# Row sums of a two-layer graph network folded and turned by VectorE instead of TensorE

## The reference

```
h = relu(layernorm(x))
x = x + adj @ (h * (u >= 0.1) / 0.9)
h = relu(layernorm(x))
x = x + adj @ (h @ W) + b
```

## Time and profile before

| what | us |
|---|---|
| median of 3 runs | 932.2 (932.02 to 932.36) |
| the profiled execution's own time | 932.63 |
| its span, first to last instruction | 930.8 |
| TensorE busy | 900.5 (97%) |
| VectorE busy | 175.6 (19%) |
| ScalarE busy | 23.8 (3%) |
| loads of `adj`, 340 of 1 MB | 391 GB/s on average over the span |

### The profile page before, as it was taken

How to read it: one execution, slowest core, us unless ns; L and a number is a source line. 1 busy time by engine, 2 the same in 40 slices (tenths; PEclk the granted TensorE clock), 3 DMA queues, 4 the chain that set the end, 5 groups by cost and what they waited for, 6 DMA issues and landing times.

```text
span 930.8 us, 10203 instructions
## 1 busy us (share of the span) xinstructions
PE 900.5 (97%) x4480; PEld 356.8 (38%) x4480; DVE 175.6 (19%) x343; ACT 23.8 (3%) x52; POOL 35.6 (4%) x32
## 2 busy tenths in 40 slices
PE   2789999999999999999999999999999999999998
PEld 0224333333334444444444444444444444444444
DVE  5513123132022112021200100200100100200223
ACT  2100000000000000000000000000000000000000
POOL 5900000000000000000000000000000000000000
PEclk9999999999999999999999999999999999999999
DMA  9999999999999999999999999899999999999993
GB/s 370 421 421 421 421 421 421 421 421 420 421 422 421 421 421 420 421 418 404 395 391 359 347 381 395 324 374 352 362 346 376 366 415 400 370 358 421 386 423 155
DMA packets 50828, 363.55 MB, mean 391 GB/s; under 512 B 5680, under 2 KB 5712, under 8 KB 6752
## 3 DMA queue, kind: packets, MB, share of 16 engines
q1 hardware_dynamic: 50688, 362.83, 96.8%
q0 software_dynamic: 96, 0.07, 0.0%
HBM read 360.78 MB, written 2.10 MB: 390 GB/s over the span
## 4 chain that ended last, share of the span: by engine, by line
PE 89%; DMA 10%; SPq 1%; issue 0%; DVE 0%; DVEq 0%
PE banks L583 47%; PE row_sums L572 36%; DMA blocks<-in_adj 10%; PE banks L578 4%; PE turned L643 1%; SPq L363 1%; PE turned L630 1%; SPq L357 0%; SPq L356 0%; DVE rows L532 0%; DVEq L274 0%
## 5 line engine op out<-in xcount | busy, mean ns | idle before, releaser
L583 PE MATMUL banks<-blocks,features 128*64 128x512 f32 x2048 | 670.0, 592 | 1.2 <-DMA blocks<-in_adj 1.2
L572 PE MATMUL row_sums<-blocks,features 128*64 128x512 f32 x1880 | 604.9, 596 | 25.9 <-DMA blocks<-in_adj 25.7
L583 PEld LDWEIGHTS banks<-blocks,features 128*64 128x64 f32 x2048 | 226.6, 137 | 261.9 <-issue 261.9
L572 PEld LDWEIGHTS row_sums<-blocks,features 128*64 128x64 f32 x1880 | 197.7, 138 | 272.2 <-issue 260.8
L509 DVE TENSOR_TENSOR acc<-acc,banks 128x512 f32<-128x512 f32 (+1 forms) x108 | 74.2, 687 | 625.9 <-PE banks L583 568.5
L578 PE MATMUL banks<-blocks,features 128*64 128x512 f32 x168 | 72.5, 592 | 0.0
L578 PEld LDWEIGHTS banks<-blocks,features 128*64 128x64 f32 x168 | 23.0, 137 | 24.2 <-issue 24.2
L430 ACT ACTIVATE sums_sb<-row_sums 128x512 f32<-128x512 f32 (+1 forms) x16 | 9.5, 595 | 749.8 <-PE row_sums L572 375.1
L481 DVE TENSOR_TENSOR rows<-rows,turned 128x256 f32<-128x256 f32 x16 | 6.7, 421 | 68.1 <-PE turned L630 68.1
L389 POOL TENSOR_SCALAR acc<-acc 128x512 f32<-128x512 f32 (+1 forms) x9 | 19.0, 2110 | 6.3 <-DMA acc<-in_u 5.7
L514 DVE TENSOR_TENSOR ahead<-ahead,banks 64x512 f32<-64x512 f32 x21 | 14.4, 685 | 0.7
(11 more groups left out here) (30 smaller groups left out, 72.9 us busy)
## 6 DMA issues: line engine op xcount, KB each, us to landing
blocks<-in_adj SPq DMA_DIRECT2D x340, 1024.0 KB, 10.3
rows<-in_x SPq DMA_DIRECT2D x2, 1024.0 KB, 7.7
acc<-in_u SPq DMA_DIRECT2D x2, 1024.0 KB, 9.9
out<-rows SPq DMA_DIRECT2D x8, 256.0 KB, 2.0
pair_w<-in_w POOLq DMA_DIRECT2D x2, 16.0 KB, 5.9
bias<-in_b POOLq DMA_DIRECT2D x1, 32.0 KB, 5.1
```

What stands on the lines that cost most here:

```text
L572: return nc.tensor.matmul(row_sums[at, s % 2, :], features[:, k * TILES + j, 0:D], tile_of(parts, j), start=first and t.n == row_first[s][ ...
L583: return nc.tensor.matmul(banks[at, t.sum.bank, :], features[:, t.k * TILES + j, D:2 * D], tile_of(parts, j), start=t.n == t.sum.first and ...
```

## The change

TensorE no longer folds or turns the rows of layer 1. ScalarE copies only the upper half (64 partitions) to `sums_sb`. VectorE adds the lower half to it (`folded`), transposes in squares of 32 x 32 into a PSUM bank (`squares`, which is the first bank of the former `turned`, now `finished`), and adds the squares to `rows` in eight additions of 32 partitions x 128 elements. `join_ahead` now writes into `ahead`; where the joined half is the upper one (even rows of 2 to 9), ScalarE's copy waits for it. The constant `fold` goes. `turn_pair` keeps its matmuls.

```diff
             for s in range(BLOCKS):
-                act.wait_ge(part_used, PARTS * (max(row_last[s]) + 1))
+                if s in ahead_done and s % 2 == 0:
+                    act.wait_ge(row_joined, joined_by[s])
+                    upper = ahead[D:P, s // 2 - first_ahead, :]
+                else:
+                    act.wait_ge(part_used, PARTS * (max(row_last[s]) + 1))
+                    upper = row_sums[D:P, s % 2, :]
                 if s >= 2:
-                    act.wait_ge(turned_ready, s - 1)
-
-                at = slice(s % 2 * D, s % 2 * D + D) if s in ahead_done else slice(0, P)
-                nc.scalar.activation(sums_sb[at, s % 2, :], row_sums[at, s % 2, :], ACT.Copy).then_inc(row_copied, 1)
+                    act.wait_ge(row_folded, s - 1)
+                nc.scalar.activation(sums_sb[:, s % 2, :], upper, ACT.Copy).then_inc(row_copied, 1)
...
-                bank = turned[:, s % 2, 0:TILES * D].rearrange("p (t d) -> p t d", d=D)
-                dve.wait_ge(turned_ready, s + 1)
-                nc.vector.tensor_tensor(mine, mine, bank, ALU.add).then_inc(turned_taken, 1)
-                dve.wait_ge(turned_taken, s + 1)
+                dve.wait_ge(row_copied, s + 1)
+                dve.wait_ge(part_used, PARTS * (max(row_last[s]) + 1))
+                lower = row_sums[0:D, s % 2, :]
+                if s in ahead_done:
+                    dve.wait_ge(row_joined, joined_by[s])
+                    if s % 2 == 1:
+                        lower = ahead[0:D, s // 2 - first_ahead, :]
+                if s:
+                    dve.wait_ge(row_turned, s)
+                nc.vector.tensor_tensor(folded[:, :], lower, sums_sb[:, s % 2, :], ALU.add).then_inc(row_folded, 1)
+                dve.wait_ge(row_folded, s + 1)
+                if s:
+                    dve.wait_ge(row_placed, s * (D // SQ) * (P // SQ))
+                nc.vector.transpose(squares, folded[:, :]).then_inc(row_turned, 1)
+                dve.wait_ge(row_turned, s + 1)
+                for f in range(D // SQ):
+                    part = squares[f * SQ:(f + 1) * SQ, :].rearrange("p (t a f) -> p t a f", t=TILES, f=SQ)
+                    for a in range(P // SQ):
+                        to = mine[a * SQ:(a + 1) * SQ, :, f * SQ:(f + 1) * SQ]
+                        nc.vector.tensor_tensor(to, to, part[:, :, a, :], ALU.add).then_inc(row_placed, 1)
+                dve.wait_ge(row_placed, (s + 1) * (D // SQ) * (P // SQ))
...
-                if s >= 2:
-                    dve.wait_ge(turned_ready, s - 1)
-                nc.vector.tensor_tensor(sums_sb[at, s % 2, :], row_sums[at, s % 2, :],
-                                        ahead[at, s // 2 - first_ahead, :], ALU.add).then_inc(row_joined, 1)
+                mine = ahead[at, s // 2 - first_ahead, :]
+                nc.vector.tensor_tensor(mine, mine, row_sums[at, s % 2, :], ALU.add).then_inc(row_joined, 1)
...
             for n in range(END + 2):
                 if n < END:
                     multiply(items[n])
-                if n - 1 in row_end:
-                    turn_row(row_end[n - 1])
```

More of the change, by code:

```diff
@@ L28 @@
 BIAS_ROW = 8
+SQ = 32
 DROP = 0.1
@@ L288, in bass_gnn @@
         ahead = sb("ahead", [P, max(ahead_done) // 2 - first_ahead + 1, BLK])
-        sums_sb = sb("sums_sb", [P, 2, BLK])
-        fold = sb("fold", [P, D])
+        sums_sb = sb("sums_sb", [D, 2, BLK])
+        folded = sb("folded", [D, BLK])
         pair_w = sb("pair_w", [P, 2 * D])
@@ L309, in bass_gnn @@
         row_sums = ctx.enter_context(nc.psum_tensor("row_sums", [P, 2, BLK], f32))
-        turned = ctx.enter_context(nc.psum_tensor("turned", [P, 2, BLK], f32))
+        finished = ctx.enter_context(nc.psum_tensor("finished", [P, 2, BLK], f32))
+        squares = finished[0:D, 0, :]
         banks = ctx.enter_context(nc.psum_tensor("banks", [P, SUM_BANKS, BLK], f32))
@@ L318, in bass_gnn @@
         cleared = sem("cleared")
-        constants = sem("constants")
         warm = sem("warm")
@@ L333, in bass_gnn @@
         row_joined = sem("row_joined")
-        turned_ready = sem("turned_ready")
-        turned_taken = sem("turned_taken")
+        row_turned = sem("row_turned")
+        row_folded = sem("row_folded")
+        row_placed = sem("row_placed")
+        finished_ready = sem("finished_ready")
+        finished_taken = sem("finished_taken")
         sum_added = sem("sum_added")
@@ L367, in _ @@
                 sp.wait_ge(rows_ready, n + 1)
-                sp.wait_ge(turned_taken, BLOCKS + n + 1)
+                sp.wait_ge(finished_taken, n + 1)
                 sp.dma_start(out[:, t, :], rows[:, t, :]).then_inc(stored, 16)
@@ L374, in _ @@
             nc.gpsimd.memset(eps[:, :], EPS).then_inc(cleared, 1)
-            nc.gpsimd.memset(fold[:, :], 0.0).then_inc(cleared, 1)
             nc.gpsimd.memset(pair_w[:, :], 0.0).then_inc(cleared, 1)
[L377 to L382, removed]
+            pool.wait_ge(cleared, 2)
             pool.dma_start(pair_w[0:D, 0:D], w).then_inc(weights_arrived, 16)
@@ L527, in pair_of_rows @@
                 mine = rows[:, 2 * p * TILES:(2 * p + 2) * TILES, :].rearrange("p (r t) d -> p r t d", r=2)
-                bank = turned[:, n % 2, :].rearrange("p (t r d) -> p r t d", t=TILES, r=2)
-                dve.wait_ge(turned_ready, BLOCKS + n + 1)
+                bank = finished[:, n % 2, :].rearrange("p (t r d) -> p r t d", t=TILES, r=2)
+                dve.wait_ge(finished_ready, n + 1)
                 if n == 0:
@@ L591, in multiply @@
                     pe.wait_ge(row_copied, s - 1)
-                    if s - 2 in ahead_done:
-                        pe.wait_ge(row_joined, joined_by[s - 2])
+                    pe.wait_ge(row_folded, s - 1)
                 if s == 0:
@@ L617, in multiply @@
                     done.then_inc(part_used, 1)
[L619 to L632, removed]
             def turn_pair(p):
@@ L637, in turn_pair @@
                     pe.wait_ge(weights_arrived, 32)
-                pe.wait_ge(turned_taken, BLOCKS + n - 1)
+                    pe.wait_ge(row_placed, BLOCKS * (D // SQ) * (P // SQ))
+                if n >= 2:
+                    pe.wait_ge(finished_taken, n - 1)
                 pe.wait_ge(sum_added, closing[pair_end[p]].done)
@@ L642, in turn_pair @@
                         at, nodes = slice(half * D, (half + 1) * D), j * P + half * D
-                        done = nc.tensor.matmul(turned[at, n % 2, j * P:(j + 1) * P],
+                        done = nc.tensor.matmul(finished[at, n % 2, j * P:(j + 1) * P],
                                                 acc[:, p, nodes:nodes + D], pair_w[:, :], start=True, stop=True)
-                done.then_inc(turned_ready, 1)
+                done.then_inc(finished_ready, 1)
             for n in range(END + 2):
```

2 lines of the change are left out of this document (1 added, 1 removed).

## The result

The changed kernel takes 927.34 us (median of 4 runs, 927.01 to 927.50) against 932.28 us (4 runs, 932.02 to 932.37): ratio 0.9946, 95% interval 0.9934 to 0.9958. That is 4.9 us faster; 927.1 us was predicted. The profiled execution took 927.5 us with a span of 925.6 us.

A forecast was written before the change was run, and what follows sets the result against it. TensorE, busy 97% of the span, was taken to bound the kernel behind its last block wait at 267.81 us; 932.63 - 5.1 (eleven turns) = 927.5 us, less 0.4 to the median: 927.1 us, range 926.0 to 930.7 us.

The forecast's parts named there:

- What is removed: TensorE's sixteen turns: rows 0 to 4 give nothing, the eleven of rows 5 to 15 give 11 x 0.465 = 5.1 us.
- the block of 267.81 us: TensorE's last wait for `adj`, 0.55 us: time saved before it is lost, time saved behind it counts in full.
- The tight pair: Pair at 373.95 us: its second block lands at 372.42 us, TensorE wants it at 372.56 us; holds by 0.14 us.
- A wait for `adj` between 290 and 400 us: Sign of being wrong: the forecast expected TensorE to have no such waits.
- rival 3: Transfers take the lead back before 400 us; the 1.4 us of rows 5 to 7 turns into waits: 928.5 us, chance 0.05.
- The way to h2: From a row's end through copy, fold, transposition, eight additions and layer norm to h2: 7.74 us, 8.47 on even rows 2 to 9.
- That the wait costs nothing: Row 2: TensorE waits some 1.8 us for h2, is 1.35 us later, and regains 1.48 us by 267.81 us.
- The 1.48 us of forgiveness at 267.8 us: By 267.81 us TensorE regains turns of rows 3 and 4 (0.93 us) and the 0.55 us wait for the block.
- Rivals 1 and 2: Way to h2 longer than 7.74 us: early waits stay, 928.8 us (0.18), or slower than before, 934.4 us (0.08).
- E = 2.15 us: Excess of the way to h2 over 7.74 us at which early lateness passes the 5.1 us gain.
- Rival 4: All sixteen turns count, 16 x 0.465 = 7.4 us: 924.8 us, chance 0.04.
- Rival 5: Nothing to be seen: something else paces TensorE's stream and fills the 0.46 us; chance 0.05.

The follow-up runs named there:

- rows 0 to 2: Changed kernel with eight idle matmuls of the old turn's shape put back on TensorE for rows 0 to 2: 926.96 us, 0.9941 of before.
- rows 8 to 15: Changed kernel with eight idle matmuls per turn put back on TensorE for rows 8 to 15: 931.11 us, 0.9987 of before.
- `short`: Changed kernel, ScalarE moving the half done ahead in advance on even rows of 2 to 9, so joining and copy run together: 927.22 us, 0.9945 of before.
- `lead_7`: Changed kernel with the planner taking a row's h2 as ready 7.0 us behind the row instead of 6.0: 926.93 us, 0.9942 of before.
- the two longer ways: Changed kernel with one or four more fold-size VectorE additions before every row's transposition: 927.83 to 929.93 us with one, 938.25 us with four.
- the kernel with four additions: Changed kernel with four more fold-size VectorE additions between fold and transposition of every row: 938.25 us, 1.0064 of before.

## Why the prediction was right, step by step

- **What is removed.** Right in what a turn costs and in that early ones are free: rows 0 to 2 cost -0.2 us, rows 8 to 15 4.0 us for 3.7. The border was put at the block of 267.81 us, whose landing was taken as fixed, and there the account was off though its sum was not. In the changed kernel nothing waits there; the last wait for a block is at the pair at 372.5 us. By that border eight turns count in full and the rest adds what the pair's blocks allow, 1.48 us. The forecast had eleven turns in full. That the sums, 5.20 and 5.1 us, agree is luck in this part: the pair's blocks happened to leave 1.48 us, and the three turns of rows 5 to 7 are 1.39 us.
- **The tight pair.** Found, but with 0.14 us to spare, and TensorE waits 0.33 us. A wait for `adj` between 290 and 400 us was one of the prediction's own signs of being wrong, and this one came. It is what rival 3 names, at the size that the text gave it as "what is missing, not the whole". It takes back 0.49 us, counted from start to start, of what TensorE was ahead: 0.55 us gained at 267 us and three turns. The time 927.34 is 0.24 us over 927.1.
- **The way to h2.** Copy 0.60, fold 0.68, transposition 0.72, eight additions 2.45 us, against 0.60, 0.69, 0.69 and 2.60. To h2 it is 8.33 us for 8.47 on row 2. TensorE's wait for it was 1.57 us long at 183.09 us, put at 1.8 us and 183.40 us.
- **That the wait costs nothing.** Right, for a reason further on than the one given: `short` shortens it and `lead_7` takes it away, and neither changes the time, because waits for blocks, the last of them at the pair, take up the difference. The 1.48 us of forgiveness at 267.8 us was not there in the changed kernel: its records pass 267.26 us without a stop, where those of the kernel before ended and the wait began.
- **Rivals 1 and 2.** Their mechanism was shown with the two longer ways, but a term was missing from them. The text priced lateness as the sum of idle times; with 2.3 us of idle time the clock falls too and adds 1.5 us. So the point from which the change would have been slower is nearer than the text's E = 2.15 us, at which row 2's wait would be 1.57 + 2.15 = 3.7 us. Where exactly was not measured.
- **Rival 4** falls with the kernel that has the turns of rows 0 to 2 back. **Rival 5** falls with rows 8 to 15.

What stays open is why a block lands late. In the kernel before, a block ahead of the one at 267.81 us landed 3.95 us behind its predecessor instead of 2.49, at 255.4 us, and pushed it back; in the changed kernel's trace this came at 275 us. The traces have one to three such loads each ahead of 300 us, which land 3.0 to 4.0 us behind the one before (that of the kernel with four additions, where loads wait for slots, is left out). No run here tells what causes it. It decides whether 0.5 us shows up at one block or at another. So the border at 267.81 us was a matter of this one execution, and the forecast had no second trace of the kernel before to see that.

## What to carry to other kernels

Work taken off the busiest engine is worth what lies behind the last place where this engine waits for something else; find the tightest place for the transfers first, since the border moves there as soon as the engine gets faster. When the way to a value grows on another engine, compare it with the spare time at each place that wants the value. Row 1 had 0.46 us to spare by the forecast, and the rows behind row 5 had more than the 2.9 us of four additions, since none of them made TensorE wait. A planner's numbers that describe the old way should be set again after such a change: here two of them were worth 2.6 us, half of what the change itself brought.

## What the runs showed of the hardware

- TensorE's granted clock fell to half behind idle times of 2.30 us (with this kernel the mean clock was under full in four of five executions), 3.69 and 4.45 us, in a stream that was otherwise nearly without a gap, and stayed full behind 0.90, 1.57, 2.10 and 2.21 us (the last at row 0 of the kernel with four additions; one trace each). It was full again 3 to 4 us later; 17 records behind the three waits took 5.62, 5.43 and 5.67 us instead of 4.08 us, so each fall cost 1.4 to 1.6 us. Idle matmuls in the gap kept it full.
- The start of the kernel looks like a half clock too, though the clock has no record there: behind 16.40 us without work the first 24 records of the changed kernel took 6.91 us, where at 0.43 us a pair they would take 5.3 us. In the kernel before, 32 took 9.61 us for 7.0. So the clock was not full throughout, as was written above. TensorE still waits for blocks behind this stretch (0.55 and 0.34 us at the next ones), so it is not a part of the difference between the two kernels.
- VectorE's additions to another group of 32 partitions start only when the one before has ended (0.31 us apart for 0.28 us long), additions to the same group start 0.07 us before its end.
- A transposition in squares of 32 x 32 of 64 x 512 f32 from SBUF to PSUM takes 0.72 us, as long as an addition of that size (0.68 us) and 0.04 us.
